# A third dA tile and a later, regrouped start of each turn in a Mamba, attention and mixture-of-experts kernel

## The reference

```python
x = x + mamba(group_norm(x), ...)       # per joint a scan over time: h = exp(dt*A)*h + dt*u*B, y = sum_s h*C
t = tokens(x)
t = t + relu(attn(ln(t)) @ proj_w + b)  # 8 heads of 16, 800 x 800 softmax
f = ln(t)
# each sample picks 2 of 8 experts by the mean of its tokens
t = t + layer_norm(sum_k w_k * (gelu(f @ W1_k + b1_k) @ W2_k + b2_k) + f) * gamma + beta
```

## Time and profile before

| | us |
|---|---|
| three runs | 1881.63, 1883.83 (median), 1887.71 |
| profiled execution, its own time | 1886.02 |
| its span | 1884.4 |
| busy: PE, DVE, ACT, POOL | 1201.0, 1397.6, 1086.1, 699.1 |
| dbu of step 0, turns 1 to 7 | 200.83, 399.76, 595.58, 791.89, 988.12, 1185.41, 1382.28 |
| experts' stage, from the last transposes of turn 8 | 1708 to 1884.4 |

### The profile page before, as it was taken

How to read it: one execution, slowest core, us unless ns; L and a number is a source line. 1 busy time by engine, 2 the same in 40 slices (tenths; PEclk the granted TensorE clock), 3 DMA queues, 4 the chain that set the end, 5 groups by cost and what they waited for, 6 DMA issues and landing times. The chain is left out here.

```text
span 1884.4 us, 21877 instructions
## 1 busy us (share of the span) xinstructions
PE 1201.0 (64%) x7072; PEld 516.5 (27%) x7072; DVE 1397.6 (74%) x2336; ACT 1086.1 (58%) x1985; POOL 699.1 (37%) x399
## 2 busy tenths in 40 slices
PE   4125377845785578547863887378837773884982
PEld 2002122332223222322231323132322232222762
DVE  4896788778886888789787977788878873502675
ACT  3333557674767478737873686567665753663330
POOL 2363335323552355235524453335324540000344
PEclk9556688877997689868995899588968896896996
DMA  2430623054304531363127120713064305004441
GB/s 56 158 131 27 189 57 127 15 185 88 132 27 166 107 124 36 141 132 114 45 81 192 60 99 32 212 48 132 12 195 85 124 18 105 2 1 117 136 125 35
DMA packets 88348, 182.19 MB, mean 97 GB/s; under 512 B 15442, under 2 KB 42894, under 8 KB 88238
## 3 DMA queue, kind: packets, MB, share of 16 engines
q1 hardware_dynamic: 85950, 174.27, 31.8%
q0 software_dynamic: 1408, 3.29, 0.6%
q10 hardware_dynamic: 880, 3.28, 0.6%
HBM read 143.61 MB, written 36.86 MB: 96 GB/s over the span
## 5 line engine op out<-in xcount | busy, mean ns | idle before, releaser
L1183 DVE TENSOR_TENSOR_SCAN hst<-dA,PS 128x800 f32<-128x800 f32 x256 | 466.2, 1821 | 142.2 <-ACT dA L880 74.9
L921 ACT ACTIVATE probs<-PS 128x400 f32<-128x400 f32 x800 | 342.0, 523 | 104.1 <-PE PS L1486 103.0
L880 ACT ACTIVATE dA<-dt_rep,a_sb 128x775 f32<-128x775 f32 x256 | 242.2, 951 | 173.3 <-DVE hst L1183 167.7
L1486 PE MATMUL PS<-q_stack,k_stack 99*128 99x400 bf16 (+1 forms) x896 | 236.5, 358 | 88.8 <-ACT probs L921 46.3
L1176 DVE TENSOR_TENSOR PS<-u_rep,b_rep 128x800 f32<-128x800 f32 x256 | 268.0, 1047 | 15.4 <-DMA u_rep<-u_dram 4.5
L911 ACT ACTIVATE probs<-PS 128x400 f32<-128x400 f32 x400 | 201.8, 504 | 133.1 <-PE PS L1453 111.0
L1210 DVE CUSTOM_DVE_ANT_0 probs<-PS,probs 128x400 f32<-128x400 f32 x400 | 220.3, 574 | 42.3 <-PE PS L1458 17.2
L1471 PE MATMUL PS<-probs,v_ext 128*32 128x400 f32 (+1 forms) x1792 | 203.4, 532 | 14.5 <-DVE o_raw L1231 8.9
L759 POOL TENSOR_TENSOR dt_sb<-hst,c_rep 128x800 f32<-128x800 f32 x72 | 135.6, 1883 | 198.8 <-DVE PS L1176 196.0
L1452 PE MATMUL PS<-k_stack,q_stack 96*128 96x400 bf16 (+1 forms) x448 | 142.6, 354 | 95.4 <-DVE k_neg L1205 95.4
L692 POOL TENSOR_TENSOR norm_r<-norm_r,neg_half 100x8 f32<-100x8 f32 x24 | 48.8, 2031 | 371.3 <-DVE norm_r L978 353.8
(11 more groups left out here) (222 smaller groups left out, 2026.0 us busy)
## 6 DMA issues: line engine op xcount, KB each, us to landing
b_rep<-b_dram SPq DMA_DIRECT2D x64, 400.0 KB, 3.8
c_rep<-c_dram SPq DMA_DIRECT2D x64, 400.0 KB, 3.8
dt_rep<-dt_dram SPq DMA_DIRECT2D x64, 400.0 KB, 5.9
u_rep<-u_dram SPq DMA_DIRECT2D x64, 400.0 KB, 6.3
q_stack<-parts_dram SPq DMA_DIRECT2D x96, 100.0 KB, 5.1
k_stack<-parts_dram SPq DMA_DIRECT2D x96, 100.0 KB, 6.5
dt_dram<-dt_sb SPq DMA_DIRECT2D x16, 400.0 KB, 2.4
u_dram<-sp_l SPq DMA_DIRECT2D x16, 400.0 KB, 2.5
```

What stands on the lines that cost most here:

```text
L880: nc.scalar.activation(dA[:, i % 2, :].rearrange("p (j t) -> p j t", t=T)[:, :, 1:T], dt_rep[:, gi, :].rearrange("p (j t) -> p j t", t=T)[ ...
L921: nc.scalar.activation(probs[:, j % NPROB, :], bank(4 + j % 3, HALF), ACT.Exp, scale=ATT_SCALE).then_inc(probs_ready.sem, 1)
L1183: nc.vector.tensor_tensor_scan(hst[:, i % 2, :], dA[:, i % 2, :], dbu, 0.0, ALU.mult, ALU.add).then_inc(scan_done.sem, 1)
L1486: last = nc.tensor.matmul(bank(4 + j % 3, HALF)[strip], k_stack[:, h, kt * P:kt * P + strip.stop - strip.start], q_stack[:, h, q0:q0 + HAL ...
```

## The change

Five things are changed. `dA` gets a third tile. ScalarE makes three decays at the end of a front, not two, and in step i of `steps` decay i + 1, not i; it waits for scan i - 3, no longer i - 2. `ln1_tok` moves from `hst` to the storage of the probabilities, and scan 0 and scan 1 no longer wait for `ln1T_up`. The copies and `low_parts` stand two steps later (`LOW_AT` = 3), and the input norm with them (`NORM_AT` = 5). SyncE's loads for the experts are unrolled and put in another order.

```diff
-        dA = sb("dA", [P, 2, TOK])
+        NDA = 3
+        dA = sb("dA", [P, NDA, TOK])
-        ln1_tok = over(hst, NT * C, rows=TT, k=NT, c=C)
+        ln1_tok = over(probs, NT * C, rows=TT, k=NT, c=C)
-        NORM_AT = 3
+        LOW_AT = 3
+        NORM_AT = LOW_AT + 2
...
+            def load_layers(bt):
+                n, z = divmod(bt, 2)
+                sp.wait_ge(h_ready[z].sem, h_ready[z].at(n, 0))
+                experts = [nc.sync.value_load(idx[0:1, bt * TOPK + k:bt * TOPK + k + 1], min_val=0, max_val=NE - 1) for k in range(TOPK)]
+                for k, e in enumerate(experts):
+                    sp.dma_start(b1_e[z][:, k, :], ...).then_inc(e_w1_in[z].sem, 16)
+                for k, e in enumerate(experts):
+                    sp.dma_start(w1_e[z][:, k, :], ...).then_inc(e_w1_in[z].sem, 16)
+                sp.dma_start(fT_e[z], ...).then_inc(e_w1_in[z].sem, 16)
+                sp.wait_ge(e_w2_scaled[z].sem, e_w2_scaled[z].at(n, 0))
+                ...
+                return experts
+            def load_residual(bt, experts):
+                n, z = divmod(bt, 2)
+                sp.wait_ge(res_read[z].sem, res_read[z].at(n, 0))
+                ...
+            chosen = load_layers(0)
+            for bt in range(B):
+                following = load_layers(bt + 1) if bt + 1 < B else None
+                load_residual(bt, chosen)
+                chosen = following
...
-                    for i in range(2):
+                    for i in range(NDA):
                         decay(f, i)
...
-                if i >= 2:
-                    act.wait_ge(scan_done.sem, scan_done.at(m, i - 1))
+                if i >= NDA:
+                    act.wait_ge(scan_done.sem, scan_done.at(m, i - NDA + 1))
...
-                    if m is not None and i >= 2:
-                        decay(m, i)
+                    if m is not None and NDA <= i + 1 < NSTEP:
+                        decay(m, i + 1)
...
-                        elif n is not None:
-                            dve.wait_ge(ln1T_up.sem, ln1T_up.at(n, 1))
...
-                        if i in (1, 2):
-                            low_parts(i - 1)
+                        if i in (LOW_AT, LOW_AT + 1):
+                            low_parts(i - LOW_AT)
```

More of the change, by code:

```diff
@@ L641, in _ @@
             sp.wait_ge(f_out.sem, f_out.at(B, 0))
[L642 to L661, removed]
@@ new lines, in load_layers @@
+            def load_layers(bt):
[3 more added lines that the diff above has]
+                for k, e in enumerate(experts):
+                    sp.dma_start(b1_e[z][:, k, :], b1[bass.ds(e, 1)].rearrange("o p c -> (o p) c")).then_inc(e_w1_in[z].sem, 16)
+                for k, e in enumerate(experts):
+                    sp.dma_start(w1_e[z][:, k, :], w1[bass.ds(e, 1)].rearrange("o d f -> (o d) f")).then_inc(e_w1_in[z].sem, 16)
+                sp.dma_start(fT_e[z], fT_dram[bass.ds(bt, 1)].rearrange("o p f -> (o p) f")).then_inc(e_w1_in[z].sem, 16)
+                sp.wait_ge(e_w2_scaled[z].sem, e_w2_scaled[z].at(n, 0))
+                for k, e in enumerate(experts):
+                    sp.dma_start(w2_e[z][:, k, :, :], w2[bass.ds(e, 1)].rearrange("o (c p) d -> (o p) c d", p=P)).then_inc(e_w2_in[z].sem, 16)
+                return experts
@@ new lines, in load_residual @@
+            def load_residual(bt, experts):
+                n, z = divmod(bt, 2)
+                sp.wait_ge(res_read[z].sem, res_read[z].at(n, 0))
+                for k, e in enumerate(experts):
+                    sp.dma_start(b2_e[z][:, k, :], b2[bass.ds(e, 1)].to_broadcast([TT, C])).then_inc(e_f_in[z].sem, 16)
+                sp.dma_start(f_e[z].rearrange("p k c -> p (k c)"), f_dram[bass.ds(bt, 1)].rearrange("o p f -> (o p) f")).then_inc(e_f_in[z].sem, 16)
+            chosen = load_layers(0)
@@ L885, in steps @@
                 for i in range(NSTEP):
-                    if m is not None and i >= 2:
-                        decay(m, i)
+                    if m is not None and NDA <= i + 1 < NSTEP:
+                        decay(m, i + 1)
                     if n is not None:
-                        if i == 0:
+                        if i == LOW_AT - 1:
                             act.wait_ge(ln1T_up.sem, ln1T_up.at(n, 1))
@@ L893, in steps @@
                             nc.scalar.copy(lnT[:, :].rearrange("p (a t) -> p a t", a=2), halves(6)).then_inc(ln1T_ready.sem, 1)
-                        if i == 1:
+                        if i == LOW_AT:
                             act.wait_ge(q_up.sem, q_up.at(n, 1))
                             nc.scalar.copy(q_part[:, 0, :], wide(4)).then_inc(qk_first.sem, 1)
-                        if i == 2:
+                        if i == LOW_AT + 1:
                             act.wait_ge(k_up.sem, k_up.at(n, 1))
                             nc.scalar.copy(k_part[:, 0, :], wide(6)).then_inc(qk_first.sem, 1)
-                        if i == 3:
+                        if i == LOW_AT + 2:
                             act.wait_ge(v_up.sem, v_up.at(n, 1))
@@ L1179, in steps @@
                             dve.wait_ge(g_ready.sem, g_ready.at(m, i - 1))
-                        elif n is not None:
-                            dve.wait_ge(ln1T_up.sem, ln1T_up.at(n, 1))
                         dve.wait_ge(dbu_ready.sem, dbu_ready.at(m, i + 1))
-                        nc.vector.tensor_tensor_scan(hst[:, i % 2, :], dA[:, i % 2, :], dbu, 0.0,
+                        nc.vector.tensor_tensor_scan(hst[:, i % 2, :], dA[:, i % NDA, :], dbu, 0.0,
                                                      ALU.mult, ALU.add).then_inc(scan_done.sem, 1)
```

2 lines of the change are left out of this document (1 added, 1 removed).

## The result

The changed kernel takes 1861.09 us (median of four runs, 1858.87 to 1863.31); the kernel before, in four runs of the same series, 1882.73 (1880.92 to 1887.71). The ratio is 0.9883, with a 95% interval of 0.9867 to 0.9899. Five further rounds gave 0.9890 (0.9871 to 0.9909). The profiled execution has a span of 1861.7 us.

What follows compares the result with a forecast made beforehand. No single engine was taken as the bound. Turn 0 0.5, start 3.0, units 12.6, clock 2.6, turn 7 2.1 - 1.0, experts 2.5 made 22.3 us; 1883.8 - 22.3 = 1861.5, say 1862; range 1845 to 1880.

Steps and rivals of the forecast that it cites:

- rival A: Start of turns, queue: pieces and b_rep land earlier or VectorE's lead survives; 1831 us; chance 0.12.
- rival B: Units: TensorE and ScalarE make up in their next wait what VectorE frees; 1879 us; chance 0.21.
- C: Start of turns: VectorE's early steps end on a later b_rep landing; slower, 1897 us at 5 us per turn; chance 0.09.
- Start on VectorE and the queue: Turns 1 to 6: scan 0 earlier, then a stall for b_rep; k_neg 0.5 us earlier per turn, 3.0 together.
- the wall: Start of turns: b_rep of round 2, queued behind 12 pieces, lands 17.7 us behind low parts; VectorE stalls 4.4 us.
- Turn 7: Turn without input norm: 2.1 us gained in units and end, about 1.0 lost to the later b_rep landing.
- Units: Score tiles and turn end: waits for two o_raw copies go, 2.1 us per turn, 12.6 over turns 1 to 6.
- The clock: Behind the second o_raw copy: TensorE's slow clock goes in three of six turns, 0.85 us each, 2.6 together.
- Turn 8: The turn after turn 7: no gain or loss, 0 us.
- Experts: Experts' loads reordered: TensorE's first-layer wait of 2.52 us goes, 0.8 comes, clock may give 1.8; taken as 2.5 us.
- without the pause the clock may stay up: Experts, first layer of sample 1: it would take 5.54 us, not 7.33, 1.8 us more gained.

Runs made afterwards that it cites:

- third-tile run: The kernel before with only the third dA tile and each decay one step ahead: 1874.9 us, ratio 0.9957.
- start-alone run: The kernel before with only the normed input in the probabilities' tile and the start's copies, low parts and input norm two steps later: 1880.8 us, ratio 0.9974.
- experts' run: The kernel before with only the experts' loads in the new order: 1884.51 us, ratio 0.9998.
- late-copy run: The changed kernel with the second o_raw copy of a turn behind scan 23 instead of scan 22: 1897.58 us, ratio 1.0080.
- last-copy run: The changed kernel with the last o_raw copy of a turn behind dbu of step 31 instead of ahead of it: 1864.89 us, ratio 0.9890.

## Why the prediction was right, and where it was not

The forecast, 1862 us, was met within 1 us, and rivals A, B and C fell. The mechanism is the one foretold in the turns and the units; two terms were wrong and cancelled, which is luck. By its steps:

*Start on VectorE and the queue.* Right in place and size: scan 0 2.12 us behind dbu (2.1 foretold), the low parts of k at 18.9 (19.0), dbu of step 8 on the landing in each of seven turns, a stall of 3.8 in turn 4 (4.4), 7.71 to `k_neg` (7.7). One reading was off: VectorE did not run without a gap up to `k_neg` in the kernel before, it waited 0.63 us for GpSimd's power at 829.97; that wait is there in both kernels. The six turns gained 3.4 us (3.0), but no turn gained the 0.5 of the sum: it goes from a loss of 0.9 in turn 2 to a gain of 1.6 in turn 3, about the bounds that the prediction gave. The three runs that took the wall away gained what stood behind it, by three ways: another place in the queue, an earlier start of the path, work put into the stall. This is rival A's prize: it was there, and the change left it lying.

The rule cited from the Trainium skill's page DMA: Bandwidth & Descriptors, section Queues, rings and completion order, agrees with the trace: behind the 12 pieces `b_rep` needs 5.5 us to landing, ahead of them 3.5. The larger part of what the place costs is not on the rings, though: the issue itself comes 6.1 us later.

*Turn 7.* A gain of 1.1 as foretold: 2.15 in the units, less 1.13 up to `k_neg`, and 0.1 regained up to the first copy. The loss of 1.0 was met by luck: the write of `k_part` goes out 2.0 us later than before, not 0.9, as the cast ahead of it waited 1.2 us for GpSimd (last section), and the way from there to the landing was 0.8 us shorter.

*Units.* From first to last `o_raw` turn 7, which has no fall of the clock in either kernel, went from 48.89 to 46.74: 2.15 us, as the 1.27 + 0.87 of the prediction. Times six, 12.9 (12.6). The third-tile run shows that the decays alone do this, so rival B's doubt is answered. One detail was misplaced: 1.73 us came at the second copy and 0.81 at the last, and 0.39 went back in between, as the late copy had also shortened the next quarter.

*The clock.* Here the term failed: 2.6 us from three turns of six. It took the half from turn 7, where the fall was missing behind the same wait; in the start-alone run and the experts' run turn 7 has it. And it counted only falls behind this wait, and put falls elsewhere at nothing. Behind the second copy the fall went in all six turns: 5.8 us against the 15.23 that turn 7 took from second to third copy, and 0.5 from third to last in turn 1. But other falls took it back: 1.3 at the last tiles of turn 5, 1.6 more in the fronts (3.7 in turns 4 and 5, against 2.1 in turn 1 of the kernel before), 3.0 in the front of turn 8. The net is 0.4. The Trainium skill, TensorE: Matmul & The Clock Gate, section HAM oscillation, has long idle gaps of TensorE bring the slow clock. The late-copy run agrees in kind: a wait of 3.3 us brought the fall in all seven turns. That one of 1.3 us does so too, in six of seven turns in the kernel before and in 20 of 21 with the two other kernels that have it, is more than the section says; without the wait, in ten profiles, it fell in none of 70 turns.

*The clock in the fronts.* This is less clear: turns 1 and 4 do the same work in their fronts, at a clock of 1.00 and 0.51. Of the 18 fronts (turns 1 to 6) of the three profiles with two dA tiles one has a fall, of the 66 of the eleven with three dA tiles 33 have. The third-tile run alone has two, the start-alone run none, so the moved start is not what brings them. A candidate is the last copy. In 17 of the 18 fronts with two tiles it started 0.86 us behind its group, and none has a fall. The 18th is turn 1 of the kernel before: its last tiles ran slow, its copy started 0.07 us behind the group, and its front has the fall:

```profile
355.26 2.95 PE L1471 MATMUL PS<-probs,v_ext 128*32 128x400 f32 x16 [0.70 <-ACT probs L921]
...
358.28 0.58 DVE L1231 COPY o_raw<-PS 128x400 f32<-128x400 f32 x1 [0.39 <-PE PS L1471]
```

In all 66 with three tiles the copy starts 0.07 us behind. The last-copy run was to test this and did not, since its copy wasn't late; so it stays open whether the copy's start or the third decay ahead of the front matters, and why one front in two is spared.

*Turn 8.* Foretold as nothing, it lost 2.7: TensorE has the same instructions in the same order in its front, and the clock is at 0.50 from 1673 on, where in the kernel before it fell only behind the projections. The second profile of the changed kernel has no such fall there. Of the fourteen profiles eight have one, among them the start-alone run and the experts' run with two tiles, so it is scatter and not the change.

*Experts.* 2.5 foretold, 4.8 between the two profiles, of which 3.5 stands at GpSimd's first power and 1.3 in shorter pairs. But the first profile of before was an extreme one: its first layers ran for 17 us, those of three other kernels with the same order for 14.8 to 15.2. By all fourteen profiles the order is worth 0.7 to 1.5 us, by the run of it alone nothing that can be told. The term is over-sized, and its step "without the pause the clock may stay up" was wrong: in these three kernels the second layer ran at full clock behind a pause of 1.4 to 1.8 us, as it does without one (5.7 us each); the 7.33 of the earlier trace rows was the exception. And the run of the order alone is at the low clock for 6.1 us, as long as the two layers of the kernel before together (6.5).

The sum was thus met with two terms off: the clock 2.6 foretold and 0.4 found, experts 2.5 foretold and 4.8 in this pair of profiles, 3 to 4 us of which is that pair's luck.

## What to carry to other kernels

An engine that is let go earlier runs into the next landing: before moving its work, write down the path that ends in that landing and shorten that path too, here by one move in the queue's order, which was worth more than the whole change (27 us). Work that is moved should go into the stall that the move creates, not behind it. And a lateness that is paid by other engines, here 1.3 us at one copy of a turn and 0.8 at another, is found by asking which copy starts without having waited. Last, moving an instruction in its stream need not move it in time: the last-copy run was meant to make the copy late, and its start stayed 0.07 us behind the group.

## What the runs showed of the hardware

TensorE's clock is a source of scatter here: two executions of one kernel had two and five slow fronts at 1.7 to 2.0 us each, and the runs of one kernel on one chip spread over 10 us. In the fourteen profiles nine of the turns 1 to 6 have slow last score tiles (15.5 to 15.6 us from third to last copy), and in all nine the front was slow too. A term of a few us in one pair of profiles is not to be trusted without others.

VectorE's cast of a float32 tile to bfloat16 was held up in these kernels by a product that GpSimd had under way. In turn 7 of the changed kernel:

```profile
1382.10 1.93 POOL L771 TENSOR_TENSOR lnT<-hst,c_rep 128x800 f32<-128x800 f32 x1 [6.13 <-PE PS L1512]
```

```profile
1382.71 1.75 DVE L1173 CAST k_part<-part_rest 128x800 bf16<-128x800 f32 x1
```

The cast ends 0.43 us behind the product, where it takes 0.58 alone; it holds up the write of `k_part` and by that `b_rep`. The Trainium skill, SBUF — State Buffer, section SBUF: two separate sides, has a port pair that these two engines lock in turn for a whole instruction; both rows agree with it to 0.15 us. It made the write of `k_part` 0.9 to 1.7 us late where it happened in these kernels.
